# Graph layer on one core: weight preparation by chunks, and a second round in another order

## The chip, the core and the metric

The kernel runs on one core of a Trainium2 chip. The time is device microseconds of one execution, the median of several runs. The engines are TensorE (PE in the profile), VectorE (DVE), ScalarE (ACT), GpSimd (POOL) and SyncE (SP), each with its own instruction stream; they are held together by semaphores that the program waits on.

## The reference

`x` is 128 graphs of 64 nodes with 384 features, `adj` 128 x 64 x 64 of 0 and 1.

```python
h = jnp.maximum(_layernorm(x, axis=-1), 0.0)
dep_emb = dep_emb_table[dep_type_matrix]                      # dep_type_matrix = adj
hi_t = h @ W1_w[:HID] (over j) + dep_emb @ W1_w[HID:] + W1_b
hj_t = h @ W2_w[:HID] (over i) + dep_emb @ W2_w[HID:] + W2_b
relevance = jnp.sum(hi_t * hj_t, axis=-1)
masked = jnp.where(adj, relevance, NEG)
A = jax.nn.softmax(masked, axis=2)
h_syn = jax.nn.relu((A @ h) @ gcn_w + gcn_b)
out = x + (h_syn @ Wo_w + Wo_b)
```

## The kernel before

**Algebra.** With one type of edge, the scores are h M h^T plus row and column vectors and a constant, where M = W1 W2^T, and p and q (`pq_cols`) are what the type's embedding and the bias add through W1 and W2. M, `gcn_w` and `Wo` are scaled by a power of two (`scale`, from a bound on the largest value) and split into a high and a low fp16 part; so are h and all intermediate products, and each product is three fp16 matmuls (`split_product`, lines 1125 to 1138). If `adj` holds values above 1, a slow general path is taken: all engines read `has_types` and branch on it (`typed`, lines 250 to 253), with the data given here never into it.

**Tiling.** x is cut into 16 supertiles of 512 rows (8 graphs), each of four tiles k of 128 rows. For a supertile s TensorE computes G = M h^T in three chunks c (`g_chunk`), HG = h gcn_w in four tiles (`hg_tile`), the scores, the transposed attention, the aggregation Z of supertile s-1 and its output. ScalarE takes the high parts out of the banks, VectorE the low parts (`g_low_part`, `hg_low_part`, `z_low_part`), the softmax and the layernorm statistics, GpSimd the layernorm coefficients (`main_coefficients`), the low part of h (`token_low`, line 418) and the biases. Supertiles 2 and up run in a loop; supertiles 0 and 1 are written out by hand, since the weights are prepared meanwhile and h is transposed by TensorE (`early_transposes`) and not by DMA.

**The order before the loop.** Each engine works through its stream in the order written.
- TensorE (from line 1149): ten `keep_warm` matmuls of ones, the transposes of W1, six more of them as filler, the transposes of W2, M(0), p and q, M(1), the bound (three matmuls with ones, line 1195), M(2) with the column of q, the transposed norms, pair rows of W1, `early_transposes(0)`, the wide norms, pair rows of W2, p.q (line 1222), G(0), HG(0), the sum of types (line 1276) behind the first HG tile, the branch, `early_transposes(1)`, scores(0), and `second_round` (line 1398).
- ScalarE (from line 549): copies of all six transposed blocks, norms of gcn_w and Wo, high parts of M and h, four `types_above` passes over `adj` (line 488), high parts of gcn_w, evictions of G(0), then HG(0), high parts of Wo between them, the branch, its second round (line 627).
- VectorE (from line 785): largest values of W1 and W2, statistics of supertile 0, the bound with the coefficients of supertile 0 interleaved (`first_coefficients`), low parts of M and h, statistics of supertile 1, low parts of gcn_w, statistics of supertile 2, low parts of G(0) and HG(0), `has_types` (line 889), the branch, its second round (line 1072).
- GpSimd (from line 403): bias of x(0), coefficients of supertile 1, both halves of `make_bias`, coefficients of supertile 2, the branch, coefficients of supertile 3, `token_low(2)`.
- SyncE loads W1, W2, x(0), gcn_w, Wo, x(1), adj, x(2), x(3) in this order, at first without waits, and moves and transposes by DMA afterwards.

An HG tile k < 3 of supertile 1 lies in the bank of G's chunk k and waits for `g_split` (the low part of that chunk); the fourth waits for the first low part of HG (`hg_read`).

Of the kernel before, what the change touches and what calls it, by code (L numbers as in the profile page):

```python
# [5 lines left out]
def gnn_layer_program(nc, x, adj, emb, W1, b1, W2, b2, gcn_w, gcn_b, Wo, bo, out):  # L6
# [17 lines left out]
    P = 128  # L24
    GRAPHS, S, D = x.shape
# [31 lines left out]
    with ctx:  # L57
# [20 lines left out]
        w_bound = sb("w_bound", [P, DC])  # L78
        norm_part = sb("norm_part", [P, 2])
# [29 lines left out]
        def wider(slot):  # L109
# [83 lines left out]
        WARM_UP, KEEP_WARM = 10, 6  # L193
# [17 lines left out]
            w_transposed w_copied pq_projected q_copied m_done norm_made  # L211
# [12 lines left out]
         ones_made, w_transposed, w_copied, pq_projected, q_copied, m_done, norm_made,  # L224
# [98 lines left out]
        def _(pool):  # L323
# [82 lines left out]
            make_bias(0)  # L406
            make_bias(1)
            main_coefficients(2)
# [22 lines left out]

            main_coefficients(3)
            token_low(2)
# [8 lines left out]
        def _(act):  # L442
# [121 lines left out]
            for n in range(4):  # L564
                types_above(n)
# [13 lines left out]
            wo_high_part(1)  # L579
            wo_high_part(2)  # L580
# [90 lines left out]
        def _(dve):  # L671
            def statistics(s):
# [4 lines left out]
                if not isinstance(s, int) or s > 3:  # L677
                    dve.wait_ge(coef_ready, COEF_STEPS * s)
                elif s in (1, 3):

                    dve.wait_ge(coef_ready, COEF_STEPS * (s + 1) // 2)
# [4 lines left out]
            def second_statistics(tiles):  # L686

                dve.wait_ge(x1_loaded, 16)
                dve.wait_ge(coef_ready, COEF_STEPS)
                for k in tiles:  # L690
                    ins = nc.vector.bn_stats(stats6[:, k, :], x_all[:, 1, k, :])
# [12 lines left out]
            def first_coefficients():  # L704
# [6 lines left out]
                nc.vector.tensor_tensor(var, m2_e, m2_o, ALU.add).then_inc(coef_step, 1)  # L711
                dve.wait_ge(coef_step, 1)
                nc.vector.scalar_tensor_tensor(sq, gap, D / 4, gap, ALU.mult, ALU.mult).then_inc(coef_step, 1)
                dve.wait_ge(coef_step, 4)
                nc.vector.scalar_tensor_tensor(var, sq, D * EPS, var, ALU.add, ALU.add).then_inc(coef_step, 1)
                dve.wait_ge(coef_step, 5)
# [11 lines left out]
                def refine(n):  # L728
# [4 lines left out]
                times_var(0)  # L733
                dve.wait_ge(bound_wide, 1)
                nc.vector.tensor_scalar(peak[:, SC_M:SC_M + 1], pair_bank[:, BOUND, 0:1], TINY, None,
                                        ALU.max).then_inc(scale_step, 1)
                refine(0)
                peak_exponent(SC_M, SC_M + 1, 1)
                square(1)
                scale_from_exponent(SC_M, SC_M + 1, 1)  # L740
                times_var(1)
                scale_ready(SC_M, SC_M + 1, 1, m_scale_ready)
                refine(1)
                nc.vector.tensor_tensor(pq_part[:, :], pq_cols[:, 0:DC], pq_cols[:, DC:2 * DC],
                                        ALU.mult).then_inc(q_copied, 1)
                square(2)
                times_var(2)
                refine(2)
# [735 lines left out]
```

## Time and profile before

| | us |
|---|---|
| median of 3 runs (366.13 to 366.99) | 366.44 |
| the profiled execution | 366.79 |
| its span, first to last instruction | 364.9 |

| engine | busy, us | share of the span |
|---|---|---|
| TensorE, matmuls | 354.9 | 97% |
| VectorE | 263.1 | 72% |
| ScalarE | 272.9 | 75% |
| GpSimd | 178.8 | 49% |

The page says that the chain of work that ended last is to 91% TensorE's. A busy share of 97% is no proof that TensorE works at its peak, as matmuls are pipelined and their ends modelled; where its waits lie is read from the timeline. In a timeline row the first number is the start in us from the span's start, the second the length of the merged stretch, and a bracket names the idle time ahead of it and who ended it. An fp32 matmul counts as two passes.

### The profile page before, as it was taken

What the parts mean: (1) busy time and instruction counts of PE and PEld (TensorE: products, weight loads), DVE (VectorE), ACT (ScalarE), POOL (GpSimd) and SP (SyncE); (2) the same over time, 40 slices, a digit from 0 to 9 for tenths busy, and PEclk for the clock granted to TensorE, in tenths of its full rate; (3) what the DMA queues carried; (4) which work ended last, traced back from release to release, by engine and by line L of the source; (5) the groups of instructions that cost most, each with busy time, mean ns of one, the idle gap of its engine ahead of it and who ended that gap; (6) DMA issues with size and microseconds to landing.
All of it is one profiled execution on the core that took longest, in us unless ns stands there. A gap on an engine that the chain in (4) does not pass through costs nothing.

```text
span 364.9 us, 9504 instructions
## 1 busy us (share of the span) xinstructions
PE 354.9 (97%) x3144; PEld 222.5 (61%) x3144; DVE 263.1 (72%) x667; ACT 272.9 (75%) x580; POOL 178.8 (49%) x348
## 2 busy tenths in 40 slices
PE   8999879999999999999999999999999999999986
PEld 8675546565756666565756666565756666565753
DVE  1788898595867777695867777695867777586664
ACT  3499586969698787879788787879788787865742
POOL 2046871573828284654728274654728274680000
PEclk9999999999999999999999999999999999999999
DMA  7962607764649484554649384564649364444052
GB/s 225 362 208 85 175 3 141 220 115 134 176 112 232 86 249 97 178 120 145 160 104 241 86 237 108 163 132 141 167 96 249 86 172 86 116 89 143 2 154 107
DMA packets 82215, 53.87 MB, mean 148 GB/s; under 512 B 45666, under 2 KB 82148, under 8 KB 82196
## 3 DMA queue, kind: packets, MB, share of 16 engines
q1 hardware_dynamic: 81488, 53.22, 55.8%
q0 software_dynamic: 64, 0.20, 0.3%
q10 hardware_dynamic: 644, 0.20, 0.3%
q8 instruction: 11, 0.18, 0.2%
q14 instruction: 8, 0.07, 0.1%
HBM read 17.44 MB, written 12.58 MB: 82 GB/s over the span
## 4 chain that ended last, share of the span: by engine, by line
PE 91%; DVE 5%; ACT 3%; issue 1%; DVEq 0%; POOL 0%; POOLq 0%
PE bank L1135 24%; PE bank L1136 24%; PE bank L1137 24%; PE bank L1233 5%; PE bank L1376 3%; PE bank L1371 3%; PE bank L1179 2%; PE bank L1147 2%; PE bank L1342 1%; PE bank L1170 1%; PE bank L1218 1%; PE bank L1441 1%; PE bank L1443 1%; DVE wo_lo L774 1%; DVE stats L683 1%
## 5 line engine op out<-in xcount | busy, mean ns | idle before, releaser
L422 POOL TENSOR_TENSOR h_parts<-h_tok,h_parts 128x1536 f16<-128x1536 f32 (+1 forms) x14 | 41.9, 2994 | 92.7 <-ACT h_parts L467 92.7
L1135 PE MATMUL bank<-gw_hi,hT 128*128 128x385 f16 x192 | 63.1, 329 | 1.9 <-DVE g_parts L867 1.6
L398 POOL TENSOR_TENSOR x_all<-x_all,bo_all 128x1536 f32 (+1 forms) x16 | 55.1, 3450 | 16.5 <-ACT h_tok L476 16.5
L1137 PE MATMUL bank<-gw_hi,hT 128*128 128x385 f16 x192 | 62.7, 327 | 0.0
L1136 PE MATMUL bank<-gw_lo,hT 128*128 128x385 f16 x192 | 62.6, 326 | 0.0
L1135 PE MATMUL bank<-wo_hi,z_hi 128*128 128x384 f16 x180 | 58.7, 326 | 0.0
L1136 PE MATMUL bank<-wo_lo,z_hi 128*128 128x384 f16 x180 | 58.7, 326 | 0.0
L1137 PE MATMUL bank<-wo_hi,z_lo 128*128 128x384 f16 x180 | 58.7, 326 | 0.0
L1135 PE MATMUL bank<-hT,m_hi 128*128 128x512 f16 x144 | 54.6, 379 | 0.5 <-DVE hT L697 0.5
L1136 PE MATMUL bank<-hT,m_hi 128*128 128x512 f16 x144 | 54.6, 379 | 0.0
L1137 PE MATMUL bank<-hT,m_lo 128*128 128x512 f16 x144 | 54.6, 379 | 0.0
L867 DVE TENSOR_TENSOR g_parts<-bank,g_parts 128x512 f16<-128x512 f32 x48 | 33.0, 690 | 26.1 <-ACT bank L531 25.6
L538 ACT ACTIVATE z_hi<-bank,gcn_bias 128x512 f16<-128x512 f32 x48 | 33.7, 702 | 11.5 <-PE bank L1376 11.5
L526 ACT ACTIVATE g_parts<-bank,pair_bias 128x512 f16<-128x512 f32 x48 | 32.8, 684 | 12.4 <-PE bank L1137 12.4
L467 ACT ACTIVATE h_tok<-x_all,ln_add,ln_mul 128x384 f32 (+1 forms) x52 | 36.5, 701 | 6.0 <-POOL ln_add L346 6.0
L989 DVE TENSOR_TENSOR z_lo<-bank,z_hi 128x512 f16<-128x512 f32 x48 | 32.8, 683 | 9.2 <-ACT bank L540 9.2
L545 ACT ACTIVATE hg_hi<-bank 128x384 f16<-128x384 f32 x64 | 32.5, 510 | 8.6 <-PE bank L1137 8.5
L997 DVE SCALAR_TENSOR_TENSOR x_all<-bank,out_scale,x_all 128x384 f32 (+1 forms) x64 | 36.3, 609 | 1.2 <-PE bank L1447 1.1
L467 ACT ACTIVATE h_parts<-x_all,ln_add,ln_mul 128x384 f16 (+1 forms) x52 | 36.2, 697 | 0.0
L781 DVE SCALAR_TENSOR_TENSOR hg_lo<-bank,hg_hi 128x384 f16<-128x384 f32 x64 | 35.0, 547 | 0.0
L607 ACT ACTIVATE score_moved<-bank 64x256 f32<-64x256 f32 x32 | 12.1, 378 | 28.3 <-PE bank L1233 14.2
L540 ACT ACTIVATE bank<-bank,gcn_bias 128x512 f32<-128x512 f32 x48 | 32.6, 679 | 0.0
(162 smaller groups left out, 691.9 us busy)
## 6 DMA issues: line engine op xcount, KB each, us to landing
x_all<-in_x_dram SPq DMA_DIRECT2D x16, 768.0 KB, 6.1
out_dram<-x_all SPq DMA_DIRECT2D x15, 768.0 KB, 4.0
hg_parts<-hg_lo SPq DMA_DIRECT2D x32, 192.0 KB, 3.3
hg_parts<-hg_hi SPq DMA_DIRECT2D x32, 192.0 KB, 3.6
x_all<-in_L_gnn_W_w_dram SPq DMA_DIRECT2D x2, 576.0 KB, 5.0
out_dram<-x_all SPq DMA_DIRECT2D x4, 192.0 KB, 1.9
gcn_raw<-in_L_gnn_gcn_w_dram SPq DMA_DIRECT2D x1, 576.0 KB, 10.8
x_all<-in_L_gnn_Wo_w_dram SPq DMA_DIRECT2D x1, 576.0 KB, 11.3
```

Source lines behind the costliest of these rows:

```text
L398: nc.gpsimd.tensor_tensor(x_all[:, s, :, :], x_all[:, s, :, :], bo_all[:, :, :].broadcast_to([P, KT, D]), ALU.add).then_inc(x_biased, 1)
L422: nc.gpsimd.tensor_tensor(h_parts[:, tiles, 1, :], h_tok[:, tiles, :], h_parts[:, tiles, 0, :], ALU.subtract).then_inc(h_split, 1)
L467: nc.scalar.activation(to, x_all[:, s, k, :], ACT.Relu, bias=add[:, k:k + 1], scale=mul[:, k:k + 1]).then_inc(h_ready, each)
L526: nc.scalar.activation(g_parts[:, c, :, 0, :], g_bank[c], ACT.Identity, bias=pair_bias[:, c:c + 1], scale=PROJ).then_inc(g_high, 1)
L538: nc.scalar.activation(z_hi[:, c, :], z_bank, ACT.Relu, bias=gcn_bias[:, c:c + 1], scale=Z_DOWN).then_inc(z_high, 1)
L781: nc.vector.scalar_tensor_tensor(hg_lo[:, k, :], bank[hg_banks(s)[k]][:, 0:D], PROJ, hg_hi[:, k, :], ALU.mult, ALU.subtract).then_inc(hg_s ...
L867: nc.vector.tensor_tensor(g_parts[:, c, :, 1, :], g_bank[c], g_parts[:, c, :, 0, :], ALU.subtract).then_inc(g_split, 1)
L989: nc.vector.tensor_tensor(z_lo[:, c, :], z_bank, z_hi[:, c, :], ALU.subtract).then_inc(z_split, 1)
L997: nc.vector.scalar_tensor_tensor(x_all[:, s, k, :], bank[O_BANK[k]][:, 0:D], out_scale[:, 0:1], x_all[:, s, k, :], ALU.mult, ALU.add).then ...
L1135: nc.tensor.matmul(dst, lh, rh, start=(c == 0), stop=False)
L1136: nc.tensor.matmul(dst, lh, rl, start=False, stop=False)
L1137: last = nc.tensor.matmul(dst, ll, rh, start=False, stop=(c == DC - 1))
```

## The change

- TensorE: no filler between the transposes. M(0) is computed chunk by chunk as the copies of W1 and W2 come. p and q stand after the first third of M(1), M(2) ahead of the bound; the bound and p.q are one matmul each with a column sum that VectorE makes. The pair rows stand around `early_transposes(0)`. The sum of types stands ahead of the fourth HG tile instead of behind the first.
- ScalarE: no copies of W2. One `types_above` ahead of gcn_w, one behind each eviction of a G(0) chunk. The high parts of Wo move to the second round.
- VectorE: copies W2. Half of the statistics of supertile 0 ahead of p and q, half behind. The bound's steps are interleaved with the first coefficients. Two added reductions to column sums. `g_low(0, 0)` ahead of the statistics of supertile 2. The second round in another order.
- GpSimd: `make_bias(1)` behind the coefficients of supertile 2, `token_low(2)` ahead of the coefficients of supertile 3.

```diff
@@ gpsimd @@
             make_bias(0)
+            main_coefficients(2)
             make_bias(1)
-            main_coefficients(2)
...
+            token_low(2)
             main_coefficients(3)
-            token_low(2)
@@ scalar @@
-            for c in range(DC):
-                act.wait_ge(w_transposed, DC + c + 1)
-                nc.scalar.activation(w2T[:, c, 0:D], bank[3 + c][:, 0:D], ACT.Copy).then_inc(w_copied, 1)
             gcn_norm()
             wo_norm()
             m_high_part(0)
+            early_normalise(0, range(EARLY_WIDE, KT))
             m_high_part(1)
-            early_normalise(0, range(EARLY_WIDE, KT))
+            early_high_part(0, 0)
             m_high_part(2)
-            for c in range(DC):
-                early_high_part(0, c)
+            early_high_part(0, 1)
+            early_high_part(0, 2)
             act.wait_ge(consts_made, 1)
-            for n in range(4):
-                types_above(n)
+            types_above(0)
...
                 g_high_part(0, c)
                 g_whole(c)
+                types_above(c + 1)
             hg_high_part(0, 0)
-            wo_high_part(0)
             hg_high_part(0, 1)
             early_normalise(1, range(0, EARLY_WIDE))
             hg_high_part(0, 2)
-            wo_high_part(1)
-            wo_high_part(2)
             hg_high_part(0, 3)
...
                 for c in range(DC):
                     early_high_part(1, c)
+                for c in range(DC):
+                    wo_high_part(c)
                 move_scores(0)
@@ vector @@
+            for c in range(DC):
+                dve.wait_ge(w_transposed, DC + c + 1)
+                nc.vector.tensor_copy(w2T[:, c, 0:D], bank[3 + c][:, 0:D]).then_inc(w2_copied, 1)
...
-            statistics(0)
+            part_statistics(0, range(0, 2))
             dve.wait_ge(pq_projected, 1)
...
+            part_statistics(0, range(2, KT))
             first_coefficients()
...
+                dve.wait_ge(top_step, 5)
+                nc.vector.tensor_reduce(bound_sum[:, :], w_bound[:, :], AX.X, ALU.add).then_inc(bound_ready, 1)
...
+            dve.wait_ge(top_step, 6)
+            nc.vector.tensor_reduce(pq_sum[:, :], pq_part[:, :], AX.X, ALU.add).then_inc(q_copied, 1)
...
+            g_low_part(0, 0)
             statistics(2)
-            for c in range(DC):
-                g_low_part(0, c)
+            g_low_part(0, 1)
+            g_low_part(0, 2)
+            early_normalise(1, range(EARLY_WIDE, KT))
...
             def second_round():
-                early_low_part(1, 0)
+                for c in range(DC):
+                    early_low_part(1, c)
+                dve.wait_ge(bias_made, 1)
+                masked_scores(0)
+                g_low_part(1, 0)
+                part_statistics(3, range(0, 2))
+                attention(0, prev=False)
+                third_mean_made()
+                g_low_part(1, 1)
                 wo_low_part(0)
-                early_low_part(1, 1)
+                attention_high(1, prev2=False)
                 wo_low_part(1)
-                early_low_part(1, 2)
-                dve.wait_ge(bias_made, 2)
-                masked_scores(0)
-                wo_low_part(2)
-                statistics(3)
-                third_mean_made()
-                g_low_part(1, 0)
-                attention(0, prev=False)
-                g_low_part(1, 1)
+                part_statistics(3, range(2, KT))
                 shared_high_parts(2)
-                attention_high(1, prev2=False)
                 g_low_part(1, 2)
                 shared_low_parts(2)
+                wo_low_part(2)
+                dve.wait_ge(bias_made, 2)
                 aggregated(1)
@@ tensor @@
-                if n == 0:
-                    keep_warm(KEEP_WARM, 7)
...
-            pe.wait_ge(w_copied, 2 * DC)
-            m_block(0, D)
+            for c in range(DC):
+                pe.wait_ge(w_copied, c + 1)
+                pe.wait_ge(w2_copied, c + 1)
+                last = m_step(0, c, D)
+            last.then_inc(m_done, 1)
+            m_step(1, 0, D)
...
-            m_block(1, D)
+            m_step(1, 1, D)
+            m_step(1, 2, D).then_inc(m_done, 1)
+            pe.wait_ge(q_copied, 2)
+            for c in range(DC):
+                last = m_step(2, c, D + 1)
+            last.then_inc(m_done, 1)
             pe.wait_ge(bound_ready, 1)
...
+            nc.tensor.matmul(pq_bank[:, BOUND, :], ones[:, :], spread(bound_sum[:, :]), start=True,
+                             stop=True).then_inc(bound_wide, 1)
...
-                if k == 0:
+                if k == 2:
 
                     pe.wait_ge(type_sums, 4)
```

## Rows read from the trace of the kernel before

**Rows 1.** Timeline of TensorE, 0 to 56 us: start, length (us), engine, line, tiles, count, [idle before].

```profile
1.17 4.64 PE L1147 MATMUL bank<-ones 128*128 128x128 f32 x20 [1.17 <-POOL ones L326]
...
6.98 1.50 PE L1147 MATMUL bank<-ones 128*128 128x128 f32 x12
...
10.16 2.20 PE L1179 MATMUL bank<-x_all 128*128 128x384 f32 x6 [0.69 <-ACT x_all L554]
...
24.17 0.38 PE L1135 MATMUL bank<-hT,m_hi 128*128 128x512 f16 x1
...
30.00 0.33 PE L1135 MATMUL bank<-gw_hi,hT 128*128 128x385 f16 x1
...
36.13 1.47 PE L1170 MATMUL bank<-ident,h_tok 128*128 128x128 f32 x12
...
39.48 0.38 PE L1135 MATMUL bank<-hT,m_hi 128*128 128x512 f16 x1
...
47.65 0.34 PE L1135 MATMUL bank<-gw_hi,hT 128*128 128x385 f16 x1 [1.37 <-DVE g_parts L867]
...
55.00 0.34 PE L1135 MATMUL bank<-gw_hi,hT 128*128 128x385 f16 x1 [0.33 <-DVE hg_lo L781]
```

**Rows 2.** The load of W2 (line 286), issued at 1.23 us: time to landing.

```profile
DMA to landing us min/median/max: 6.0/6.0/6.0
```

**Rows 3.** Timeline of VectorE, 16 to 35 us.

```profile
16.29 0.16 DVE L735 TENSOR_SCALAR peak<-bank 128x1 f32<-128x1 f32 x1 [0.69 <-PE bank L1195]
...
21.00 0.69 DVE L697 SCALAR_TENSOR_TENSOR hT<-bank,hT 128x512 f16<-128x512 f32 x1 [0.42 <-ACT hT L481]
...
24.37 0.17 DVE L839 COPY pair_all<-bank 128x6 f32<-128x6 f32 x1 [0.30 <-PE bank L1222]
...
25.27 0.21 DVE L847 TENSOR_SCALAR gcn_bias<-gcn_raw,scale 128x3 f32<-128x3 f32 x1
...
34.50 0.13 DVE L889 TENSOR_SCALAR has_types<-type_top 1x1 int32<-1x1 f32 x1
```

**Rows 4.** Timeline of ScalarE, 18 to 30 us.

```profile
18.32 1.30 ACT L476 ACTIVATE h_tok<-x_all,ln_add,ln_mul 128x384 f32<-128x384 f32 x2
...
21.82 1.16 ACT L492 ACTIVATE x_all<-adj_all,const_all 128x1024 f32<-128x1024 int32 x1
...
28.05 0.68 ACT L526 ACTIVATE g_parts<-bank,pair_bias 128x512 f16<-128x512 f32 x1
...
29.19 0.68 ACT L526 ACTIVATE g_parts<-bank,pair_bias 128x512 f16<-128x512 f32 x1
```

**Rows 5.** Timeline of VectorE, 44 to 55 us.

```profile
44.27 0.61 DVE L774 SCALAR_TENSOR_TENSOR wo_lo<-x_all,scale,wo_hi 128x384 f16<-128x384 f32 x1
...
44.80 1.93 DVE L683 BATCH_NORM_STATS2 stats<-x_all 128x6 f32<-128x384 f32 x4
...
49.57 0.86 DVE L1057 TENSOR_SCALAR h_tok<-x_all,third_mean 128x384 f32<-128x384 f32 x2
...
51.01 0.59 DVE L984 COPY attT_hi<-bank 64x256 f16<-64x256 f16 x2
...
53.66 0.69 DVE L989 TENSOR_TENSOR z_lo<-bank,z_hi 128x512 f16<-128x512 f32 x1 [0.28 <-ACT bank L540]
```

**Rows 6.** Timeline of ScalarE, 49 to 53 us.

```profile
49.56 0.60 ACT L597 ACTIVATE attT_parts<-bank 128x512 f16<-128x512 f16 x1 [1.17 <-PE bank L1342]
...
51.79 0.71 ACT L467 ACTIVATE h_parts<-x_all,third_add,third_mul 128x384 f16<-128x384 f32 x1
```

**Rows 7.** GpSimd's two long passes (timeline), the masks of line 1004 (timeline, then by line).

```profile
54.50 1.65 POOL L422 TENSOR_TENSOR h_parts<-h_tok,h_parts 128x768 f16<-128x768 f32 x1
...
319.90 6.84 POOL L398 TENSOR_TENSOR x_all<-x_all,bo_all 128x1536 f32<-128x1536 f32 x2
...
325.39 1.73 DVE L1004 TENSOR_SCALAR masks<-adj_all,row_term 128x64 f32<-128x64 f32 x3
...
L1004 DVE TENSOR_SCALAR masks<-adj_all,row_term x64: 238/247/1409, 41.4 to 346.5; 128x64 f32 x48, 128x64 f32<-128x64 f32 x16
```

More of the change, by code:

```diff
@@ L684, in statistics, with part_statistics @@
                 ins.then_inc(stats_ready, 1)
-            def second_statistics(tiles):
-                dve.wait_ge(x1_loaded, 16)
-                dve.wait_ge(coef_ready, COEF_STEPS)
+            def part_statistics(s, tiles):
+                if s == 0:
+                    dve.wait_ge(x_loaded, 16)
+                elif s == 1:
+                    dve.wait_ge(x1_loaded, 16)
+                    dve.wait_ge(coef_ready, COEF_STEPS)
+                else:
+                    dve.wait_ge(x_loaded, 16 * s)
+                    dve.wait_ge(coef_ready, COEF_STEPS * 2)
                 for k in tiles:
-                    ins = nc.vector.bn_stats(stats6[:, k, :], x_all[:, 1, k, :])
+                    ins = nc.vector.bn_stats(stats6[:, k, :], x_all[:, s, k, :])
                 if tiles[-1] == KT - 1:
@@ L835, in _ @@
                                     ALU.max).then_inc(scale_step, 1)
-            second_statistics(range(0, 1))
+            early_low_part(0, 2)
+            part_statistics(1, range(0, 1))
             peak_exponent(SC_WO, SC_GCN + 1, 5)
@@ L844, in _ @@
             scale_ready(SC_WO, SC_GCN + 1, 5, scale_step)
-            second_statistics(range(1, 2))
+            part_statistics(1, range(1, 2))
             dve.wait_ge(scale_step, 9)
@@ L1175, in spread, with m_step, pair_row @@
                 return column.broadcast_to([column.shape[0], SPREAD])
-            def m_block(d, columns):
+            def m_step(d, c, columns):
+                return nc.tensor.matmul(bank[d][:, 0:columns], w1T[:, c, d * P:(d + 1) * P], w2T[:, c, 0:columns],
+                                        start=(c == 0), stop=(c == DC - 1))
+            def pair_row(e):
                 for c in range(DC):
-                    last = nc.tensor.matmul(bank[d][:, 0:columns], w1T[:, c, d * P:(d + 1) * P], w2T[:, c, 0:columns],
-                                            start=(c == 0), stop=(c == DC - 1))
-                last.then_inc(m_done, 1)
-            pe.wait_ge(w_copied, 2 * DC)
-            m_block(0, D)
+                    last = nc.tensor.matmul(pair_bank[:, 1 + e, :], w2T[:, c, e * P:(e + 1) * P],
+                                            spread(pq_cols[:, DC + c:DC + c + 1]), start=(c == 0), stop=(c == DC - 1))
+                return last
+            for c in range(DC):
[4 more added lines that the diff above has]
+            m_step(1, 0, D)
             pe.wait_ge(dep_loaded, 16 * 4)
@@ L1191, in _ @@
             last.then_inc(pq_projected, 1)
-            m_block(1, D)
-            pe.wait_ge(bound_ready, 1)
-            for c in range(DC):
-                last = nc.tensor.matmul(pair_bank[:, BOUND, :], ones[:, :], spread(w_bound[:, c:c + 1]),
-                                        start=(c == 0), stop=(c == DC - 1))
-            last.then_inc(bound_wide, 1)
-            pe.wait_ge(q_copied, 2)
-            m_block(2, D + 1)
-            pe.wait_ge(norm_made, 2)
-            for n in range(2):
-                last = nc.tensor.transpose(bank[6][0:1, n * P:(n + 1) * P], norm_part[:, n:n + 1], ident[:, :])
-            last.then_inc(norm_rows, 1)
-            pe.wait_ge(scale_step, 1)
+            m_step(1, 1, D)
[4 more added lines that the diff above has]
+            last.then_inc(m_done, 1)
+            pe.wait_ge(bound_ready, 1)
+            nc.tensor.matmul(pq_bank[:, BOUND, :], ones[:, :], spread(bound_sum[:, :]), start=True,
+                             stop=True).then_inc(bound_wide, 1)
             for e in range(DC - 1):
@@ L1210, in _ @@
                                      spread(pq_cols[:, c:c + 1]), start=(c == 0), stop=(c == DC - 1))
+            pe.wait_ge(norm_made, 2)
+            pe.wait_ge(scale_step, 1)
+            for n in range(2):
+                last = nc.tensor.transpose(bank[6][0:1, n * P:(n + 1) * P], norm_part[:, n:n + 1], ident[:, :])
+            last.then_inc(norm_rows, 1)
+            pair_row(0)
             early_transposes(0)
@@ L1214, in _ @@
                              stop=True).then_inc(norms_wide, 1)
-            for e in range(DC):
-                for c in range(DC):
-                    nc.tensor.matmul(pair_bank[:, 1 + e, :], w2T[:, c, e * P:(e + 1) * P],
-                                     spread(pq_cols[:, DC + c:DC + c + 1]), start=(c == 0), stop=(c == DC - 1))
+            pair_row(1)
+            pair_row(2)
             pe.wait_ge(q_copied, 3)
-            for c in range(DC):
-                last = nc.tensor.matmul(pair_bank[:, 0, :], ones[:, :], spread(pq_part[:, c:c + 1]),
-                                        start=(c == 0), stop=(c == DC - 1))
-            last.then_inc(pairs_done, 1)
+            nc.tensor.matmul(pair_bank[:, 0, :], ones[:, :], spread(pq_sum[:, :]), start=True,
+                             stop=True).then_inc(pairs_done, 1)
             def scores_of(s, half):
```

58 lines of the change are left out of this document (28 added, 30 removed).

## The prediction

> **What bounds the kernel now.** I read the timeline of TensorE first. From the first projection to the last output it is a nearly unbroken stream, and all its waits but the start and the end lie before 56 us, so the change, which touches only the weight preparation, supertile 0 and the second round, moves the end by as much as it moves the point where TensorE last waits: the last hg tile of supertile 1, which starts at 55.00 after a wait for VectorE's `hg_lo` [rows 1]. From there on the loop is TensorE's own. So I follow the change to that point. Earlier waits there are small: 0.69 us before M, 1.37 us before the first hg tile of supertile 1.
>
> **First part, up to the scales.** W2 landed at 1.23 + 6.0 = 7.23 us [rows 2], while TensorE, done with W1 at about 7.0, ran twelve filler passes until 8.32 (6.98 plus 1.34) [rows 1]. Without them W2's transposes start at about 7.3, one microsecond earlier. VectorE then copies its blocks. No VectorE copy of 128x384 fp32 from a bank is among these rows; it lies between 0.48 (1.93/4, statistics of as many elements in SBUF) and 0.69 us (`z_lo`, 128x512 from a bank) [rows 5], and I take 0.55, since it reads a bank, but fewer elements. M begins after the first copy, at 8.5 in place of 10.16, and its later copies come at 0.5 us, faster than TensorE uses them (two passes of 0.34 each). That M no longer waits for six copies is the gain.
>
> It does not reach the scale of M. M(2) now stands ahead of the bound's matmul: 18 M passes (0.33 each) and 12 of p and q (0.11) from 8.5 end at 15.9, and VectorE reads the bound at about 16.3, as before (16.29) [rows 3]. What does gain is the layernorm chain: its dependent steps of 0.2 us are worked off while VectorE waits for the bound, so the coefficients are ready at 17.25 and not 18.2. ScalarE, after its first `m_hi`, starts its two `h_tok` at 17.75 and not 18.32 [rows 4]: 0.6 earlier, and with them the transposes of supertile 0 and VectorE's work from 21.00 on. A gap of 0.3 to 0.4 before the pair copy (24.37) goes too, because the column sums cut twelve passes to four and G(0) follows them at 22.5, 1.7 us earlier than 24.17. VectorE's `gcn_bias` at 25.27 comes at 24.3 [rows 3], so the weight scales are ready at 24.5.
>
> **Second part, the decision on types.** Every engine passes a branch on `has_types`. Before, it was computed at 34.50, and TensorE's next instruction, the transposes of supertile 1, started 1.63 later, at 36.13 [rows 1, 3]. That is its register load and branch: the stream has a small gap there that nothing else explains. ScalarE sets it now. Before, its four passes over the types (1.13 each) filled the time before `gw_hi`. Now one of them does, from 21.7 to 22.85, and ScalarE idles until 24.5. Then it has in one unbroken row: the `gw` conversions, 28.05 - 21.82 - 4 x 1.13 = 1.71; three pairs of G evictions, 29.19 - 28.05 = 1.14 each; and the other three type passes: 1.71 + 3.42 + 3.39 = 8.5, until 33.05 [rows 4]. An `hg_hi` (0.5) and two row terms with their low parts (1.3, by the 1.34 us between 53.66 and 55.00, less one `z_lo`) follow: `has_types` at 34.85, the transposes at 36.5, 0.35 us later than before. What was 1.7 us ahead at G(0) is behind here.
>
> **Third part, the second round.** From the transposes to G(1) it is 39.48 - 36.13 = 3.35 us, and G without waits 30.00 - 24.17 = 5.83 [rows 1]. The three low parts of h now stand first on VectorE, so G(1) has no waits and ends at 36.5 + 9.2 = 45.7. The scores of supertile 0 reach the exponentials some 2 us earlier than before, and `g_low(1, 0)` stands behind them at about 43.2, so the wait of 1.37 us before 47.65 is gone. ScalarE copies the transposed attention 49.56 - 47.65 = 1.91 after the start of that tile [rows 1, 6]: at 47.6 in place of 49.56. VectorE, free since about 47.65, begins `attT_hi` at 48.25 instead of 51.01: 2.75 us gained.
>
> Now the queue behind it. Before, 3.99 us lay between `attT_hi` (51.01) and TensorE's tile (55.00), 0.28 of them idle: 3.7 of work. The new order puts in front of the same point two `wo_lo` (0.53 each: the next instruction starts at 44.80 after 44.27), half of the statistics (0.93 of 1.93), and the shared high parts (51.01 - 49.57 = 1.44) [rows 5]. That is 3.4 more, 7.1 in all, and the tile starts at 48.25 + 7.1 = 55.35. TensorE waits twice, 2 us for `g_low(1, 2)` and over 1 us for `hg_lo`. Balance: 0.35 us late.
>
> **Fourth part, GpSimd.** `token_low(2)` used to run at 54.50 for 1.65 us, after the coefficients of supertile 3. It now stands before them, and starts as soon as ScalarE has written its second tile of supertile 2, 51.79 + 0.71 - 49.56 = 2.94 after the attention copy: at 50.65 [rows 6, 7]. At that moment VectorE is in its shared high parts, from 50.35 to 51.8: four `tensor_scalar` from SBUF to SBUF. The only case in the trace of such an instruction under a long pass of GpSimd is a mask at 325.39: it took 1409 ns against a median of 247, and its end is that of GpSimd's pass, 319.90 + 6.84 = 326.74 [rows 7]. [...] Bounds: nothing, if GpSimd gets in only behind them; 1.65, if at once. I take 1.5, by the mask. The small coefficient steps that now come later cost nothing: statistics and `normalise(3)` have several us.
>
> The Trainium skill, SBUF — State Buffer, section "SBUF: two separate sides", says that VectorE in a two-port mode and GpSimd lock their shared ports for a whole instruction and that the later one stands still. The trace agrees in the mask's 1409 ns; by the page the low parts, which read two SBUF operands, would be held as well. The sum is the same without the page.
>
> **Sum.** 0.35 + 1.5 = 1.85 us later: the tile starts at 56.85. The profiled execution took 366.79 us with a span of 364.9, 0.35 above the median of 366.44. I expect a span near 366.8 and a median of 366.44 + 1.85 = **368.3**. A measurement of this kernel can tell 0.2%, 0.73 us, from no change.
>
> **Rivals.**
> (a) *The ports don't meet.* GpSimd's pass starts a little after the high parts or is held by them, or its hold is short. For it: the stretched mask is a single case, of another shape. Then only the queue is left: 366.8, within 0.2%. The same result comes if the decision on types is up to 0.7 us earlier than I have it and the ports meet only in part.
> (b) *The gain of the start comes through*, the case on the other side. The place is ScalarE's row before `has_types`. My 24.5 for the weight scales follows the transposes of h; G(0) itself is 1.7 earlier. If the scales had all of that lead they would be ready at 23.8, 0.7 earlier than I have them; and if TensorE's branch, with its queue empty, costs 1.2 and not 1.63, the transposes start 1.1 to 1.2 earlier. Each tenth counts one to one up to the last tile, since no later step has slack against it. With no port conflict that is 366.8 - 1.2 = 365.6, and it decides from transposes before 35.4. Against it: the row is 8.5 us of ScalarE work with its durations all in the trace.
> (c) *The clock.* The first twenty passes took 4.64 us, 0.23 each; the fillers at 6.98 took 1.34 for twelve, 0.11 [rows 1]. That is the step from 1.2 to 2.4 GHz, though the granted clock reads 1.0 there. Without fillers TensorE idles 0.1 to 0.3 us between 7.1 and 8.5. If the clock fell there, M and p, q would take up to 5 us more: 370 and above. The stream before idled 0.69 at 9.5 and stayed fast, so this is small.
> (d) *p, q wait for their inputs.* They started behind M(0), 10.16 + 2.0, and now want to start a microsecond earlier. Bound: 0 to 0.8 us for M(2), shifting all. It is inside the range.
>
> **Chances.** Ports meet, slower by 1 to 2.5 us: 0.50, (c) and other losses 0.04; (a), within 0.2%: 0.27; (b), faster: 0.19. Faster by over 0.2%: 0.19; within: 0.27; slower: 0.54. The range takes in the queue alone, most of (b), and the full port hold with 0.7 us of error in the hand-made schedule: 365.4 to 369.1. The forecast's own range is 367.5 to 369.1.
>
> **What would show it.** G(0) at 22.5; `has_types` at 34.85 and the transposes of supertile 1 at 36.5; no wait before the first hg tile of supertile 1; waits of about 2 us or more before its third and of over 1 before its fourth tile; one VectorE `h_tok` or `h_parts` of 1.5 us or more beside `token_low(2)`; the fourth tile at 56.85. The forecast is wrong if the fourth tile starts before 55, if no `tensor_scalar` is stretched, or if TensorE waits anywhere after it.

## The result and the profile after

The changed kernel takes 370.1 us (median of 5 runs, 369.41 to 370.94) against 366.44 us, a ratio of 1.0099 with a 95% interval of 1.0086 to 1.0112: 3.7 us slower. The profiled execution took 369.41 us with a span of 367.5; it is the fastest of the five, and that matters below. Line numbers are those of the changed kernel: its helper `split_product` has lines 1147 to 1149, `early_transposes` 1180, the scores 1248.

Timeline of TensorE after (columns as in [rows 1]):

```profile
5.59 3.17 PE L1168 MATMUL bank<-ident,x_all 128*128 128x128 f32 x18
8.85 2.82 PE L1188 MATMUL bank<-x_all 128*128 128x384 f32 x8
...
22.54 0.38 PE L1147 MATMUL bank<-hT,m_hi 128*128 128x512 f16 x1
...
36.63 1.50 PE L1180 MATMUL bank<-ident,h_tok 128*128 128x128 f32 x12 [1.48 <-DVE hg_lo L794]
...
40.23 0.22 PE L1248 MATMUL bank<-hT,g_parts 128*128 128x64 f16 x2 [0.75 <-issue]
40.35 0.38 PE L1147 MATMUL bank<-hT,m_hi 128*128 128x512 f16 x1
...
54.29 0.34 PE L1147 MATMUL bank<-gw_hi,hT 128*128 128x385 f16 x1 [3.38 <-DVE g_parts L877]
...
55.77 0.53 PE L1147 MATMUL bank<-gw_hi,hT 128*128 128x385 f16 x1
56.09 0.53 PE L1148 MATMUL bank<-gw_lo,hT 128*128 128x385 f16 x1
...
57.06 0.50 PE L1147 MATMUL bank<-gw_hi,hT 128*128 128x385 f16 x1
...
60.47 0.33 PE L1147 MATMUL bank<-wo_hi,z_hi 128*128 128x384 f16 x1
```

M starts at 8.85 and G(0) at 22.54; in [rows 1] they stand at 10.16 and 24.17. At the transposes of supertile 1 the lead has turned into 0.50 us of delay (36.63 against 36.13), at the fourth hg tile it is 2.06 us (57.06 against 55.00), at the output of supertile 0, which began at 57.88 in the kernel before, 2.59 us. The span is 2.6 us longer, so nothing is lost or won after that.

The new thing is the pitch of the passes between 54.8 and 58 us: 0.32 us from start to start (55.77 to 56.09), where such passes follow each other at 0.16 elsewhere. Busy time by stretch (TensorE, its weight loads, VectorE, ScalarE, GpSimd; then the granted clock, DMA share, GB/s) says why:

```profile
50.00:54.00 4.00, 0.91 (x24) 0.78 (x21) 4.00 (x7) 4.00 (x9) 2.63 (x5) 1.00 0.00 0
54.00:55.00 1.00, 0.71 (x4) 0.46 (x5) 1.00 (x3) 1.00 (x3) 0.80 (x3) 0.88 0.00 0
55.00:56.00 1.00, 1.00 (x5) 0.46 (x3) 1.00 (x3) 0.22 (x1) 1.00 (x1) 0.50 0.00 0
56.00:57.00 1.00, 0.94 (x3) 0.15 (x1) 1.00 (x4) 0.02 (x1) 0.75 (x4) 0.50 0.35 81
57.00:58.00 1.00, 0.94 (x3) 0.43 (x4) 1.00 (x4) 0.47 (x1) 0.70 (x4) 0.50 1.27 290
58.00:59.00 1.00, 1.00 (x7) 0.63 (x6) 1.00 (x4) 0.00 (x0) 0.71 (x4) 0.91 1.24 283
```

The granted clock was 0.50, the lower level of 1.2 GHz, from just before 55 to past 58 us, after TensorE had stood for 3.38 us. Before 54 and after 59 it is 1.00. The stretch also shows that VectorE is busy without a pause from 50 to 59 us: it is the bound here.

VectorE after, from the copy of the attention on (the answer to [rows 5]), with GpSimd's pass:

```profile
48.71 0.60 DVE L995 COPY attT_hi<-bank 64x256 f16<-64x256 f16 x2 [0.42 <-ACT attT_parts L594]
49.34 0.62 DVE L787 SCALAR_TENSOR_TENSOR wo_lo<-x_all,scale,wo_hi 128x384 f16<-128x384 f32 x1
49.87 1.01 DVE L693 BATCH_NORM_STATS2 stats<-x_all 128x6 f32<-128x384 f32 x2
50.80 2.17 DVE L1068 TENSOR_SCALAR h_tok<-x_all,third_mean 128x384 f32<-128x384 f32 x2
52.89 0.74 DVE L1073 TENSOR_SCALAR h_parts<-h_tok,third_mul 128x384 f16<-128x384 f32 x2
53.55 0.68 DVE L877 TENSOR_TENSOR g_parts<-bank,g_parts 128x512 f16<-128x512 f32 x1
```

```profile
51.10 1.66 POOL L424 TENSOR_TENSOR h_parts<-h_tok,h_parts 128x768 f16<-128x768 f32 x1 [5.40 <-ACT h_parts L469]
```

The two `h_tok` took 2.17 us where [rows 5] has 0.86, under GpSimd's pass, which now runs at 51.10 and not at 54.50 [rows 7]. Next comes the low part of G(1)'s last chunk, for which TensorE stands.

### The profile page after: what moved, and what is told of

It reads as the page before. It is cut to its first block, busy times and chain, and to the rows that moved or that the text cites. A ratio compares the mean times of both kernels' runs of the same rounds, so it can differ in the third digit from the quotient of the medians.

```text
span 367.5 us, 9472 instructions
## 1 busy us (share of the span) xinstructions
PE 354.2 (96%) x3124; PEld 221.6 (60%) x3124; DVE 266.0 (72%) x672; ACT 272.0 (74%) x577; POOL 178.1 (48%) x348
## 4 chain that ended last, share of the span: by engine, by line
PE 84%; DVE 7%; ACT 2%; issue 2%; DMA 2%; POOL 2%; DVEq 0%; SPq 0%; ACTq 0%; POOLq 0%
PE bank L1147 23%; PE bank L1148 23%; PE bank L1149 23%; PE bank L1248 6%; PE bank L1391 3%; PE bank L1386 3%; DMA x_all<-in_L_gnn_W_w_dram 2%; DVE stats L693 1%; PE bank L1357 1%; POOL root_sq L348 1%; ACT h_tok L478 1%; PE bank L1180 1%; PE bank L1456 1%; PE bank L1458 1%; ACT bank L610 0%
## 5 line engine op out<-in xcount | busy, mean ns | idle before, releaser
L1147 PE MATMUL bank<-gw_hi,hT 128*128 128x385 f16 x192 | 63.7, 332 | 3.5 <-DVE g_parts L877 3.4
L1149 PE MATMUL bank<-gw_hi,hT 128*128 128x385 f16 x192 | 63.4, 330 | 0.0
L469 ACT ACTIVATE h_tok<-x_all,ln_add,ln_mul 128x384 f32 (+1 forms) x52 | 36.5, 702 | 5.5 <-POOL ln_add L348 5.5
L533 ACT ACTIVATE bank<-bank,pair_bias 128x512 f32<-128x512 f32 x48 | 31.5, 655 | 0.0
```

The source lines that it names most:

```text
L469: nc.scalar.activation(to, x_all[:, s, k, :], ACT.Relu, bias=add[:, k:k + 1], scale=mul[:, k:k + 1]).then_inc(h_ready, each)
L1147: nc.tensor.matmul(dst, lh, rh, start=(c == 0), stop=False)
L1149: last = nc.tensor.matmul(dst, ll, rh, start=False, stop=(c == DC - 1))
```

## The experiments

The theory after the two traces: the 3.7 us are (1) a VectorE queue that is longer ahead of the low parts TensorE waits for, (2) 1.31 us that GpSimd's pass holds VectorE, and (3) a lower clock of TensorE behind its wait. Rivals: that the clock costs nothing, as TensorE waits for VectorE there anyway; that the loss sits in the weight preparation or in ScalarE's row before `has_types`.

**Filling the wait (e3).** `summed` and `score_copied` are waited for, so that the bank of the filler is free.

```
     aggregation(1, Z_BANK)
+    pe.wait_ge(score_copied, GT)
+    pe.wait_ge(summed, GT)
+    keep_warm(14, 6)
     for k in range(2, KT):
```

> The changed kernel, but TensorE runs fourteen fp32 matmuls of ones (28 passes, 3.1 us) into a free bank while it waits for the third hg tile of supertile 1. Nothing else moves. Theory: the clock stays up, the third tile takes 1.5 us and not 2.6, the fourth starts at 57.0 as before but takes 1.5 and not 2.0: 368.6. Rival (the clock fell for another reason than the idle time, or its fall costs nothing since VectorE is late anyway): 370.1.

368.71 us (368.35 to 369.18, 4 runs), ratio 1.0064 (1.0043 to 1.0084), as the theory had it. TensorE and the granted clock in this kernel:

```profile
50.53 3.37 PE L1159 MATMUL bank<-ones 128*128 128x128 f32 x28
54.09 0.34 PE L1147 MATMUL bank<-gw_hi,hT 128*128 128x385 f16 x1 [0.18 <-DVE g_parts L877]
...
56.86 0.34 PE L1147 MATMUL bank<-gw_hi,hT 128*128 128x385 f16 x1 [1.13 <-DVE hg_lo L794]
```

```profile
54.00:56.00 2.00, 1.65 (x9) 0.80 (x9) 2.00 (x5) 1.24 (x3) 1.79 (x3) 1.00 0.04 8
56.00:58.00 2.00, 1.14 (x7) 0.70 (x8) 2.00 (x7) 0.26 (x1) 1.42 (x8) 1.00 0.95 177
```

The fourth tile still waits for the same `hg_lo` and starts at nearly the same time, 56.86, but the clock stays at 1.00, and the kernel is 370.1 - 368.7 = 1.4 us faster. That is the price of the lower clock, as a median over few runs: the intervals of the two ratios only just part (1.0086 against 1.0084), and 0.20 us of the gain in the profiled execution is its earlier fourth tile. The price lies behind the fourth tile: the slow passes of the third tile end before `hg_lo` anyway.

The traces show it without a median. From the start of the fourth tile to the output of supertile 0 it is 2.88 us in the kernel before, 2.89 in this one and 3.41 in the changed kernel, whose profiled execution had a mean clock of 0.995. In the profiled executions of e1, e2 and e5 below, with means of 0.990 and 0.991, it is 4.84, 5.16 and 5.42 us. The fourth tile, the output and the clock in that of e2:

```profile
56.84 0.50 PE L1147 MATMUL bank<-gw_hi,hT 128*128 128x385 f16 x1 [4.46 <-DVE hg_lo L794]
...
62.00 0.33 PE L1147 MATMUL bank<-wo_hi,z_hi 128*128 128x384 f16 x1
```

```profile
58.00:60.00 2.00, 2.00 (x12) 1.04 (x11) 1.16 (x3) 0.04 (x1) 1.45 (x8) 0.50 0.82 183
60.00:62.00 2.00, 2.00 (x48) 2.00 (x45) 1.33 (x6) 0.45 (x1) 0.09 (x1) 0.59 0.00 0
```

So the lower clock cost 0.5 us where it was over soon after 58 us, and 2.0 to 2.5 us where it lasted to about 61 us or longer.

**GpSimd's pass out of VectorE's shared parts (e1).** It now waits until all four shared high parts are written.

```
+    pool.wait_ge(coef_step, 22)
     token_low(2)
     main_coefficients(3)
```

> The changed kernel, but GpSimd's token_low(2) waits until VectorE's four high parts of supertile 2 are done. Theory (ports, long queue, clock): the pair of h_tok passes takes 0.87 us again and not 2.17, the fourth hg tile of supertile 1 starts at 55.7 and not 57.06, TensorE's wait before the third tile is 2.1 us and not 3.4. If the clock then stays up: 367.1 us. If it falls after 2.1 us too: 368.6. Rival (the two passes only happened to be long, the ports are not the cause): no change, 370.1.

369.47 us (367.48 to 370.14, 9 runs), ratio 1.0062 (1.0042 to 1.0082), and the runs fall into groups by their mean granted clock: at 1.00 they took 367.48, 367.74 and 367.78 us, at 0.99 369.48 to 370.14, the two at 0.995 lie between (368.22 and 369.47). Both groups are above what was expected of them (367.1 and 368.6). In the profiled execution, one of 0.99:

```profile
53.03 0.34 PE L1148 MATMUL bank<-gw_hi,hT 128*128 128x385 f16 x1 [2.07 <-DVE g_parts L878]
...
56.82 0.50 PE L1148 MATMUL bank<-gw_hi,hT 128*128 128x385 f16 x1 [1.71 <-DVE hg_lo L795]
```

The wait of 3.38 us became 2.07 us, 1.31 less, what `h_tok` had been stretched by. But the shared low parts, which VectorE does later, then met the pass instead (2.15 us for the two, 1.14 in the changed kernel), and TensorE has a second wait of 1.71 us: the hold has moved, and the fourth tile comes only 0.24 us earlier (56.82 against 57.06). With two shorter waits the clock fell in some executions and not in others, and between the medians of the two groups lie 2.1 us. So the clock is worth more here than the 1.31 us of the hold.

**Both together (e6).** The edit above and `keep_warm(9, 6)` ahead of the third tile.

> e1 and e3 together: GpSimd's token_low(2) waits for the high parts, and TensorE runs nine matmuls of ones (18 passes, 2.0 us) while it waits for the third tile. Theory: no fall of the clock in any run, so one time and not two groups, that of e1's fast group: 367.5. Against e3 (368.7) that gives the cost of the ports alone, 1.2. Rival (e1's spread has another cause than the clock): two groups again, median 369.

368.94 us (367.89 to 369.90, 5 runs), ratio 1.0068 (1.0045 to 1.0091): a miss. Now the third tile starts without a wait, but a wait of 2.1 us stands ahead of the fourth, and the mean clock was 1.00 in two runs (368.22 and 367.89 us) and 0.994 to 0.995 in three (368.94 to 369.90). The fourth tile starts at 56.85, close to the 56.86 of e3 and the 56.82 of e1. The filler kept the clock over the wait that it filled; behind the wait of 2.1 us that was left, the clock fell at times.

**The low part of G ahead of the statistics and the shared high parts (e2).**

```
     wo_low_part(1)
+    g_low_part(1, 2)
     part_statistics(3, range(2, KT))
     shared_high_parts(2)
-    g_low_part(1, 2)
```

> The changed kernel, but g_low(1, 2) stands ahead of the second half of the statistics and of the high parts. Theory: the third hg tile follows the aggregation at 50.8 without a wait, but the fourth still waits for the same VectorE queue, so the idle time only moves behind the third tile (4.7 us) and the clock falls there: 369.5 to 370.5. Rival (what costs is the low part of G standing last in the queue): with that wait gone the loss is gone, 366.7 or less.

370.02 us (369.70 to 370.84, 4 runs), ratio 1.0094 (1.0076 to 1.0113), as expected. TensorE no longer waits ahead of the third tile, but 4.46 us ahead of the fourth, which starts at 56.84 (57.06 in the changed kernel). The end is set by the whole queue ahead of `hg_lo`, not by the place of one step in it.

**The queue shortened (e4).** In the second round VectorE does the shared parts at once, the low parts of Wo one by one behind `z_lo`, and the half of the statistics of supertile 3 behind all of them.

```
     g_low_part(1, 1)
-    wo_low_part(0)
+    shared_high_parts(2)
     attention_high(1, prev2=False)
-    wo_low_part(1)
-    part_statistics(3, range(2, KT))
-    shared_high_parts(2)
     g_low_part(1, 2)
     shared_low_parts(2)
-    wo_low_part(2)
+    wo_low_part(0)
...
         rows_and_low(s, c)
+        if first and c < 2:
+            wo_low_part(c + 1)
+        elif first:
+            part_statistics(3, range(2, KT))
```

> The changed kernel with another VectorE second round: shared high parts in the idle time before attT_hi, g_low(1, 2) right behind attT_hi, low parts of Wo and the second half of the statistics between the z low parts. Theory (the length of the queue ahead of the fourth tile decides): third tile at 51.2 without a long wait, fourth at 53.5 in place of 57.06 and 55.00 before; no fall of the clock; 364.9. Rival (start-up work of the other engines sets the end, or the shared low parts meet GpSimd's pass at 51.1 and are held): 366.3 or more.

369.0 us (368.73 to 369.32, 4 runs), ratio 1.0071 (1.0052 to 1.0091): a miss by 4 us. The fourth tile starts at 54.28, before the 55.00 of [rows 1], so the queue term is real. Two things took its place. VectorE and GpSimd:

```profile
51.03 2.00 DVE L787 SCALAR_TENSOR_TENSOR wo_lo<-x_all,scale,wo_hi 128x384 f16<-128x384 f32 x1
```

```profile
50.63 1.99 POOL L424 TENSOR_TENSOR h_parts<-h_tok,h_parts 128x768 f16<-128x768 f32 x1 [4.86 <-ACT h_parts L469]
```

`wo_lo` is held for 1.4 us, and GpSimd's own pass is longer too, 1.99 for 1.66 us. And ScalarE and TensorE further on:

```profile
65.09 0.71 ACT L469 ACTIVATE h_tok<-x_all,ln_add,ln_mul 128x384 f32<-128x384 f32 x1 [1.26 <-POOL ln_add L348]
```

```profile
71.87 0.34 PE L1148 MATMUL bank<-gw_hi,hT 128*128 128x385 f16 x1 [2.60 <-DVE g_parts L877]
```

The late statistics make the coefficients of supertile 3 late, ScalarE's layernorm stands for them with the high parts of G(2) queued behind it, and TensorE waits 2.60 us at 71.87. The mean clock was 1.00 in two executions and 0.995 and 0.994 in the others, against what was expected, but their times don't differ (369.16 and 368.85 us against 369.32 and 368.73). The point "all waits lie before 56 us" holds only while that chain has its time.

**The statistics early (e7).** As the last one, with the statistics directly behind `shared_low_parts(2)` and `wo_low_part(c)` behind each row c.

> e4, but the second half of the statistics of supertile 3 stands right behind the shared low parts, so that its coefficients aren't late, and all three low parts of Wo stand behind the hg low parts, clear of GpSimd's pass. Theory (e4 gained at the fourth tile and lost it when ScalarE's normalise(3) waited for the coefficients until 65.09): fourth tile at 53.3, no wait of TensorE after it, but ScalarE's normalise(3) ends only about 1 us earlier than in the kernel before, which bounds the gain: 365.3. Rival (the loss of e4 has another cause): 368.5 or more.

366.2 us (365.94 to 366.64, 10 runs), ratio 0.9994 (0.9983 to 1.0005). All of the loss is gone, with the weight preparation, the order of the types and of GpSimd as in the changed kernel. So the loss came in by VectorE's second round, and the rivals by which it sits in the weight preparation or in ScalarE's row fall. The same place in this trace:

```profile
50.33 1.14 DVE L1080 SCALAR_TENSOR_TENSOR h_parts<-h_tok,third_mul,h_parts 128x384 f16<-128x384 f32 x2
51.38 1.01 DVE L693 BATCH_NORM_STATS2 stats<-x_all 128x6 f32<-128x384 f32 x2
```

```profile
50.99 1.99 POOL L424 TENSOR_TENSOR h_parts<-h_tok,h_parts 128x768 f16<-128x768 f32 x1 [4.89 <-ACT h_parts L469]
```

```profile
53.63 0.34 PE L1146 MATMUL bank<-gw_hi,hT 128*128 128x385 f16 x1 [0.96 <-DVE hg_lo L794]
...
57.59 0.34 PE L1146 MATMUL bank<-wo_hi,z_hi 128*128 128x384 f16 x1 [0.91 <-DVE wo_lo L787]
```

GpSimd found VectorE in a low part and was itself the one that took longer, 1.99 for 1.66 us. Then the statistics run beside its pass in their usual 1.01 us; where e4 has a `wo_lo` at this place, it was held. TensorE waits twice for under 1 us, and the clock stays. The time is 0.9 us above what was expected. The fourth tile is 1.37 us ahead of [rows 1], the output only 0.29 (57.59 against 57.88), with the 0.91 us of waiting in between that was not expected.

**The order of the types (e5, and e8 with the order of e7).** Two passes over the types ahead of the high parts of gcn_w, the others behind the first two evictions of G(0), and none behind the third.

```
     types_above(0)
+    types_above(1)
     for c in range(DC):
         gcn_high_part(c)
...
     g_whole(c)
-    types_above(c + 1)
+    if c < 2:
+        types_above(c + 2)
```

> The changed kernel, but two of the four type passes stand ahead of gw_hi on ScalarE, in the 1.65 us that it idles there, and the other two behind the evictions of the first two G(0) chunks. Theory (the decision on types waits for ScalarE's unbroken row): has_types comes at 34.0 and not 35.07, the transposes of supertile 1 at 35.5 and not 36.63, and all of it reaches the end: 369.0. Rival (another gate, the coefficients of supertile 1 or the hg tiles, is right behind): under 0.4 us, 369.8.

> e7 with the two type passes of e5 ahead of gw_hi. Theory: the gains add: 364.2. Rival (the second round is bound by ScalarE or GpSimd by now): no better than e7, 365.3.

The first alone: 369.06 us (368.23 to 371.2, 5 runs), ratio 1.0056 (1.0034 to 1.0078); with the order of e7 too: 366.18 us (365.85 to 366.96, 10 runs), ratio 0.9990 (0.9980 to 0.9999), 2 us above what was expected of it and no better than e7. `has_types` in the changed kernel, then `has_types` and the transposes in the first one's trace:

```profile
35.07 0.13 DVE L901 TENSOR_SCALAR has_types<-type_top 1x1 int32<-1x1 f32 x1
```

```profile
34.94 0.13 DVE L903 TENSOR_SCALAR has_types<-type_top 1x1 int32<-1x1 f32 x1
```

```profile
36.50 1.50 PE L1182 MATMUL bank<-ident,h_tok 128*128 128x128 f32 x12 [1.83 <-DVE hg_lo L796]
```

Though one pass of 1.13 us left ScalarE's row, `has_types` came only 0.13 us earlier, at 34.94. It stands in VectorE's queue between the low parts of HG(0), and that queue has no pause from 32.22 on (32.21 in the changed kernel). At that point VectorE has waited for ScalarE's last eviction of G(0), and the edit doesn't move it: it starts at 31.53 here and at 31.51 in the changed kernel, as the pass comes off behind it. So the pass behind the last eviction was worth a tenth; the row up to there still sets VectorE's start, and no run shortens it.

The time of the first run, 369.06 us, is the 369.0 that was expected, but by luck: the theory had `has_types` at 34.0. The mean clock was 0.995 in four of these five executions and in one of five of the changed kernel, and why isn't shown. In the trace of the second run the transposes start 0.40 us earlier than in e7 (36.65 against 37.05, 0.23 of it from an earlier start of M), but TensorE stands 1.14 us within the scores of supertile 0 where e7 has 0.22, with no releaser named. So that pair of traces doesn't show what the earlier transposes are worth.

**The filler back (e10).** e7 with the six filler matmuls of the kernel before between the transposes of W1 and W2.

```
     last.then_inc(w_transposed, 1)
+    if n == 0:
+        keep_warm(6, 7)
```

> e7 with the six fp32 filler matmuls back between the transposes of W1 and W2: one part of the change undone. Theory of the prediction (the filler cost 1 us of TensorE's start, but the chain of supertile 0 hangs on VectorE's bound and the coefficients, which stayed at 16.1 to 16.3): the transposes of W2 start at 8.3 to 8.6 instead of 7.96, M(2) and the scale of M come up to 0.6 us later, and the time is 366.2 + 0 to 0.6, so 366.5. Rival (the start counts for nothing, since has_types hangs on ScalarE's row behind the weight scales): 366.2. Rival on the other side (the filler keeps the early passes fast): the passes of M are shorter than in e7 and the time is below 366.

367.12 us (366.40 to 367.69, 10 runs), ratio 1.0013 (1.0002 to 1.0024). M starts at 9.43 and not at 8.85 (the changed kernel) or 9.25 (e7, where W2 landed late), and the transposes of supertile 1 at 37.20 (37.05 in e7). That the start counts one to one up to the transposes is shown by all traces with this weight preparation: W2 landed at different times, M starts at 8.85 to 9.43, and the transposes follow it by 27.77 to 27.82 us in eight traces, and by 27.63 or 27.64 in the three with two passes over the types ahead of gcn_w. So the rival by which the start counts for nothing falls. The size at the end is not shown. Against e7's 0.9994 it is 0.7 us, but the intervals of the two overlap, and of the 0.64 us by which the fourth tile is later in the traces (54.27 against 53.63) only 0.15 are there at the transposes; within the scores of supertile 0 TensorE then stands 0.55 us longer (0.77 against 0.22), with no releaser named.

**One more order (e9).** e8 with the statistics behind the first rows, and the low parts of Wo ahead of the rows of tiles 1 and 2.

> The second round of e7 reordered once more, with the types of e5: behind the first z_lo and rows come the statistics and wo_lo(0), behind the second z_lo come wo_lo(1) and wo_lo(2), and the rows of tiles 1 and 2 come behind the third z_lo. In e7's trace the fourth tile waited 0.96 us for the first hg_lo, with 0.93 us of statistics ahead of it, and the output waited 0.91 us for wo_lo(2), with a row term and an hg_lo of 0.65 us and more ahead of it. Theory (each step off VectorE's queue ahead of a point where TensorE waits comes through one to one): the fourth tile starts 0.9 us earlier against the start of supertile 1 than in e7, the output 1.1 us earlier, and the time is 366.2 - 1.1 = 365.1 us; ln_add of supertile 3 comes 1.3 us later than in e7 and nobody waits for it. Rival (the time is held further on, by ScalarE's normalise of supertile 3 and the low parts of G behind it): TensorE waits near 70 us and the time stays at 366.2.

366.95 us (366.59 to 367.29, 11 runs), ratio 1.0007 (0.9998 to 1.0016): no gain over e8, by the ratios 0.6 us slower, with intervals that just touch. TensorE:

```profile
53.49 0.34 PE L1156 MATMUL bank<-gw_hi,hT 128*128 128x385 f16 x1 [0.80 <-DVE hg_lo L796]
...
57.28 0.32 PE L1156 MATMUL bank<-wo_hi,z_hi 128*128 128x384 f16 x1 [0.74 <-DVE z_lo L1002]
...
70.24 0.34 PE L1156 MATMUL bank<-gw_hi,hT 128*128 128x385 f16 x1 [0.90 <-DVE g_parts L879]
```

The output starts 0.31 us earlier than in e7 and no more, since VectorE now waits 0.67 us for ScalarE's part of Z at 52.15. And the masks of supertile 1 come at 58.82 (58.05 in e7); with them the exponentials, ScalarE's layernorm (63.46, e7 62.68) and G(2)'s parts, for which TensorE waits 0.90 us at 70.24. That is the rival's place. VectorE's whole queue up to those masks is a second bound, close behind the first. None of e7, e8 and e9 beats the kernel before by more than 0.1% (the interval of e8, 0.9980 to 0.9999, ends just short of no difference).

**GpSimd's order alone, in the kernel before (e11).**

```
-    main_coefficients(3)
     token_low(2)
+    main_coefficients(3)
```

> The kernel before with one part of the change alone: GpSimd's token_low(2) ahead of the coefficients of supertile 3. It would start when ScalarE has written its second tile of supertile 2, at 52.50, while VectorE is in its two shared low parts (52.24 to 53.30), each with two operands in SBUF. Theory (the one that holds the ports makes the other wait, instruction by instruction): GpSimd stands until the first low part ends at about 52.8, then holds the second for its 1.65 us, so a low part of 1.8 to 2.2 us, z_lo and hg_lo 1.2 to 1.4 us later, the fourth tile at 56.3, and 366.4 + 1.3 = 367.7 us. Rival (VectorE keeps the ports through both low parts, as GpSimd's 1.99 us in e7 allows): GpSimd's pass takes 2.3 to 2.5 us, no low part is stretched, and 366.4.

367.15 us (366.86 to 368.17, 10 runs), ratio 1.0022 (1.0011 to 1.0034).

```profile
51.71 2.53 DVE L1069 SCALAR_TENSOR_TENSOR h_parts<-h_tok,third_mul,h_parts 128x384 f16<-128x384 f32 x2
...
54.16 0.68 DVE L989 TENSOR_TENSOR z_lo<-bank,z_hi 128x512 f16<-128x512 f32 x1
```

```profile
52.05 1.78 POOL L422 TENSOR_TENSOR h_parts<-h_tok,h_parts 128x768 f16<-128x768 f32 x1 [5.96 <-ACT h_parts L467]
```

```profile
55.49 0.34 PE L1135 MATMUL bank<-gw_hi,hT 128*128 128x385 f16 x1 [1.34 <-DVE hg_lo L781]
```

The two low parts took 2.53 us where e7 has 1.14. The wait ahead of the fourth tile grew from 0.33 [rows 1] to 1.34 us, 1.0 us; 0.28 us of the 1.4 went into the pause that VectorE had there [rows 5]. By the ratio it is 0.8 us (0.4 to 1.2), in kind as the theory had it, a little less in size than its 1.3. That part of the change alone makes the kernel slower.

## Why the prediction was wrong

The direction was right, and the time, 370.1, lies outside the range of 365.4 to 369.1. Step by step:

**The start** was right: G(0) at 22.54 (22.5 forecast), `has_types` at 35.07 (34.85), the transposes at 36.63 (36.5), no wait ahead of the first hg tile. The 1.63 us between `has_types` and the transposes were misread, and held by luck: in the kernel before there is no gap, TensorE's own HG passes fill the time up to 36.13 (the last starts at 35.97, and they follow each other at 0.16). In the changed kernel a gap does stand there, 1.56 us from `has_types`, and it is 1.55 to 1.59 us in all eleven traces with this weight preparation. The row names VectorE's `hg_lo`, but that is no cause: it is the third one in the changed kernel and the fourth in e5, at the same distance, while the first transposes wait only for the first. So the transposes hang on `has_types`, as the prediction had it; that the time is the branch's fits and is not shown by itself. "Each tenth counts one to one" was true of the weights' chain up to the transposes (e10), not of the last pass in ScalarE's row (e5), since VectorE's queue had only 0.13 us to give. Rival (b) asked for transposes before 35.4 and fell.

**The gain at the attention** was 51.01 - 48.71 = 2.30 us, 0.46 less than forecast: 0.13 from the transposes, 0.37 from the way to G(1), 3.72 us where [rows 1] has 3.35. In it TensorE stood for 0.75 us with no releaser that the trace names.

**The queue** was right: from `attT_hi` to the fourth tile 8.35 us, of which 1.31 are the stretched `h_tok`, so 7.04 against the 7.1 of the sum.

**GpSimd's pass** was right in place, kind and, at 1.31 for 1.5 us, in size; rival (a) fell. So the fourth tile starts at 57.06, where 56.85 stood. That the hold would be 1.5 us, and not some other part of the pass's 1.65, no row of the kernel before shows: its one case is of another shape. Of the smaller sums, three don't come out as written, without effect on the forecast: the passes from 8.5 end at 15.8 and not at 15.9, 47.6 + 2.94 is 50.5 and not 50.65, and the passes of rival (c) at half the clock would take 7.3 us more, not up to 5.

**The step that failed** is the first sentence of the argument: that the end moves by as much as the point where TensorE last waits. From the fourth tile to the output it is 2.88 us in the kernel before and 3.41 here, at the lower clock. The forecast itself had TensorE wait 2 us and over 1 us, and put the hold of the port into the sum but not onto the wait, which became 3.38 us. Rival (c) looked for the clock only at the start, where nothing happened: the passes of M kept their pitch, though the filler was gone. The missing term, put at nothing, is 1.4 us by e3. In the profiled execution it is 0.53 us only. It had a mean clock of 0.995; three of the other four had 0.989 and the last 0.991, by an estimate some 7 to 8 us of lower clock (0.011 x 368 / 0.5) against nearly 4. Those four have no trace; the executions with 0.990 and 0.991 that have one (e1, e2, e5) lost 2.0 to 2.5 us there.

So of the 3.7 us, about 1.4 are the clock (e3), 1.3 the hold by GpSimd (read from `h_tok`; e11 in the other kernel has 1.0 by its trace and 0.8 by its ratio), and the rest, 1.0 by this difference (0.75 by the trace: 3.05 us more queue less 2.30 us gained at the attention), is the queue with the later start of supertile 1, where 0.35 was forecast. The split between the hold and the queue is read from the trace: no run takes the hold out of the changed kernel alone, since in e1 and e6 it only moves. "TensorE waits nowhere after the fourth tile" was true of the changed kernel, but by less of a margin than the text supposed (e4, e9).

## What to carry to other kernels

When a change gives TensorE a new wait of some microseconds in the middle of its stream, price the passes behind it at the lower clock too, and look at the granted clock there before anything else. Look at which VectorE instructions a long elementwise pass of GpSimd meets: here a pass of 1.65 us cost VectorE 1.0 to 1.4 us when it met passes from SBUF to SBUF (the changed kernel, e1, e4, e11), and nothing in the statistics of e7. Where several chains are within a few tenths of each other, taking work off one of them is worth only the distance to the next.

## What was not expected of the hardware

- The clock's fall after a wait isn't the same in each execution. The waits are those of the profiled execution, the clock is the mean of each. Behind 3.38 us of standing it fell in all five runs, for a mean of 0.989 to 0.995, and in all five of e5; behind 4.46 us (e2) in all four; behind 2.07 and 1.71 us (e1) in six of nine; behind 2.1 us (e6) in three of five; behind 1.96 and 2.60 us (e4) in two of four. Behind 1.34 us (e11) and behind two waits of 0.96 and 0.91 us (e7) the mean stayed at 0.998 and above in all ten. Most of the 2.7 us over which the times of e1 spread go with it.
- Who is held by whom is a matter of who comes first, instruction by instruction: VectorE in e4 (`wo_lo` 2.00 for 0.61 us) and in e11 (1.4 us), GpSimd in e7 (1.99 for 1.66 us), and in e4 and e11 GpSimd's pass was longer as well (1.99 and 1.78). The statistics, which read SBUF but write six values a row, ran beside the pass in their usual time; `h_tok`, which writes as much as it reads, did not. The Trainium skill, SBUF — State Buffer, section "SBUF: two separate sides", has the lock held for a whole instruction and the later engine standing; the traces agree in both directions.
- TensorE stands within the scores of supertile 0 with no releaser named, 0.48 us in the kernel before, 0.75 in the changed one, 0.22 in e7, 0.77 in e10 and 1.14 in e8. No run here shows its cause, and it is of the size of the differences between e7, e8, e9 and e10. It stays open.
